# A routed layer's results stored in slot order, gathered again by the attention behind it, and a bias moved from TensorE to VectorE

## Time and profile before

| | us |
|---|---|
| median of 3 runs | 1647.91 (1646.39 to 1648.25) |
| the profiled execution | 1648.63 |
| its span, first to last instruction | 1646.8 |

### The profile page before, as it was taken

The page is one execution under the profiler, slowest core; times in us unless marked ns, Lnnn a source line. Parts: engine busy times, 40 slices in busy tenths (PEclk is TensorE's granted clock), DMA queues, the critical chain, the costliest instruction groups (busy, mean ns, idle before and its releaser), DMA issues. The chain is left out here.

```text
span 1646.8 us, 34410 instructions
## 1 busy us (share of the span) xinstructions
PE 1358.9 (83%) x10706; PEld 1040.7 (63%) x10706; DVE 1048.7 (64%) x3598; ACT 745.1 (45%) x1519; POOL 691.5 (42%) x865
## 2 busy tenths in 40 slices
PE   3899999999849999999999556643888888299997
PEld 1566666666627888888888445532665556188886
DVE  3678777787547888888888636662788877201100
ACT  2445545455327676766767233331333333044332
POOL 2344444443300435353535438882334343234443
PEclk9999999999759999999999779986999999599999
DMA  2222122220030000000000066531400000375550
GB/s 77 34 31 39 21 37 29 28 38 16 12 103 1 17 24 19 19 23 16 26 13 26 17 214 186 174 106 51 129 27 36 29 35 31 136 253 196 182 177 11
DMA packets 65752, 108.62 MB, mean 66 GB/s; under 512 B 9767, under 2 KB 34395, under 8 KB 65296
## 3 DMA queue, kind: packets, MB, share of 16 engines
q1 hardware_dynamic: 54416, 82.27, 19.0%
q0 software_dynamic: 11264, 25.46, 4.3%
HBM read 65.34 MB, written 36.04 MB: 62 GB/s over the span
## 5 line engine op out<-in xcount | busy, mean ns | idle before, releaser
L1124 DVE TENSOR_TENSOR m_Sl<-m_S,m_Sh 128x512 fp32r<-128x512 f32 x256 | 174.3, 690 | 32.4 <-ACT m_S L1034 27.6
L1034 ACT ACTIVATE m_S<-PS,W 128x512 f32<-128x512 f32 x256 | 175.7, 686 | 25.5 <-PE PS L942 22.5
L1570 PE MATMUL PS<-f_xT,f_wt 128*128 128x256 f32 x480 | 123.3, 394 | 42.8 <-ACT f_xT L1606 42.8
L1378 POOL DMA_INDIRECT rows<-r_row,r_posi x128 | 130.5, 1019 | 35.7 <-issue 35.7
L1365 POOL TENSOR_TENSOR r_soft<-r_euler,r_soft 128x32 f32<-128x32 f32 x16 | 86.8, 5428 | 133.2 <-DVE r_soft L1270 133.2
L1029 ACT ACTIVATE m_Sh<-PS,W 128x512 fp32r<-128x512 f32 x128 | 88.2, 689 | 106.2 <-PE PS L942 105.9
L735 DVE TENSOR_TENSOR am<-PS,C 128x512 f32<-128x512 f32 x192 | 119.4, 676 | 20.9 <-PE PS L427 20.9
L1581 PE MATMUL PS<-f_wt,f_hid 128*128 128x128 f32 x960 | 130.9, 279 | 1.8 <-ACT f_hid L1619 1.8
L1655 DVE TENSOR_TENSOR f_res<-PS,f_row 128x256 f32<-128x256 f32 x40 | 17.0, 424 | 181.1 <-PE PS L1585 181.1
L1581 PEld LDWEIGHTS PS<-f_wt,f_hid 128*128 128x128 f32 x960 | 122.7, 191 | 11.1 <-ACT f_hid L1619 2.0
L1570 PEld LDWEIGHTS PS<-f_xT,f_wt 128*128 128x128 f32 x480 | 87.2, 195 | 58.5 <-ACT f_xT L1606 35.6
(11 more groups left out here) (233 smaller groups left out, 3280.9 us busy)
## 6 DMA issues: line engine op xcount, KB each, us to landing
f_row<-rows SPq DMA_DIRECT2D x80, 260.0 KB, 2.7
f_wt<-wr SPq DMA_DIRECT2D x40, 514.0 KB
f_wt<-wr SPq DMA_DIRECT2D x40, 256.0 KB, 3.1
rows<-r_padding SPq DMA_DIRECT2D x32, 260.0 KB, 3.2
X<-x SPq DMA_DIRECT2D x16, 256.0 KB, 5.6
qr<-qphi SPq DMA_DIRECT2D x64, 64.0 KB
kr<-kphi SPq DMA_DIRECT2D x64, 64.0 KB
X<-mid SPq DMA_DIRECT2D x16, 256.0 KB, 2.9
```

The costliest lines, as they stand in the source:

```text
L1034: nc.scalar.activation(S[:, n % 3, :], PS[:, n % 3, :], ACT.Silu, bias=w("b1")[:, n:n + 1]).then_inc(s_ready, 1)
L1124: nc.vector.tensor_tensor(Sl[:, n % 4, :], S[:, n % 3, :], Sh[:, n % 4, :].bitcast(F32), ALU.subtract).then_inc(sl_ready, 1)
L1378: nc.gpsimd.indirect_dma_start(out=self.rows, out_offset=bass.IndirectOffsetOnAxis(ap=self.posi[:, u, t:t + 1], axis=0), in_=self.row[:, u ...
L1570: mm = nc.tensor.matmul(PS[:, 2 + 2 * (u % 2) + bank, half * SLOT:(half + 1) * SLOT], wt[:, u, f * P:(f + 1) * P], xT[:, u % 2, :], start= ...
```

## The change

Five parts go together.

1. Layer 0's rows are 132 floats instead of 260: normalised X and the gate factor. X and the token number aren't sent; ACT's copy and DVE's copy of the number stay in layer 1 only.
2. Layer 0's results are stored in slot order by SP: in the step of slot s, SP first waits for the result of slot s-8 and stores it to rows (s-8)*256 and on of `mid`, then it issues the loads of slot s. The last 8 stores follow the loop. POOL stores nothing in this layer; DVE casts no tokens and adds beta in the closing step, without X.
3. DVE keeps each token's place (`where.row`) in `dve_place`, and at the start of the first routed layer turns it into its position in slot order (`find_tokens`, five operations).
4. The softmax attention's X stays in SBUF. POOL fetches the results of a batch by four indirect DMAs (gathers) into `G`, two batches ahead, between its two variance steps and its scatters; DVE adds G to X ahead of the statistics. SP's loads of X are gone.
5. Layer 1: b2 is part of the weights, repeated for all 128 partitions (514 KB become 578 KB a slot). The bias row's DMA, the row of ones and the two bias products a slot are gone; DVE adds row and bias into `xb` before it waits for PE, then PE's output to xb.

```diff
-ROW = 260
+ROW = (132, 260)
@@ mixture, ACT
-                    if n == 15:
-                        route(routing.act_copy_x, act, p)
@@ Routing.dve_place
+        if not self.layer:
+            nc.vector.tensor_copy(self.where.row[:, bass.ds(b * CT, CT)], self.pos[:, :])
@@ Routing.pool_scatter
-        pool.wait_ge(self.x_copied, b + 1)
+        if self.layer:
+            pool.wait_ge(self.x_copied, b + 1)
@@ routed, SP
+            def store(s, u):
+                sp.wait_ge(res_ready, s + 1)
+                sp.dma_start(dest[bass.ds(s * SLOT, SLOT), :].rearrange("(p a) d -> p a d", a=2), res[:, u, :, :]).then_inc(stored[u], 16)
+
             def step(s, u, turn):
+                if not layer and since(s, DEPTH):
+                    store(s - DEPTH if isinstance(s, int) else s + (-DEPTH), u)
                 r = sp.value_load(slot_row[0:1, bass.ds(s, 1)], min_val=0, max_val=ROWS - SLOT)
                 e = sp.value_load(slot_expert[0:1, bass.ds(s, 1)], min_val=0, max_val=EXPERTS - 1)
-                if since(s, DEPTH):
+                if layer and since(s, DEPTH):
                     sp.wait_ge(res_ready, s - (DEPTH - 1))
                 sp.dma_start(row[:, u, :, :], rows[bass.ds(r, SLOT), :].rearrange("(p a) r -> p a r", a=2)).then_inc(rows_in[u], 16)
                 sp.dma_start(wt[:, u, :], weights[bass.ds(e, 1), :, :].rearrange("o p n -> (o p) n")).then_inc(weights_in[u], 16)
-                if layer:
-                    sp.dma_start(b2r[0:1, u, :], b2[bass.ds(e, 1), :]).then_inc(weights_in[u], 16)
             over_slots(sp, step)
+            if not layer:
+                for u in range(DEPTH):
+                    store(NSLOT - DEPTH + u, u)
+                for u in range(DEPTH):
+                    sp.wait_ge(stored[u], 16 * NSLOT // DEPTH)
@@ routed, POOL
                 inverse_deviation(s, u % 2)
-                if since(s, 1):
-                    store(s - 1 if isinstance(s, int) else s + (-1), (u - 1) % DEPTH)
             over_slots(pool, step)
-            if not layer:
-                store(NSLOT - 1, DEPTH - 1)
@@ routed, PE
-                    if layer:
-                        mm = nc.tensor.matmul(PS[:, 6 + v, a * P:(a + 1) * P], one_row[:, :], b2r[0:1, u, :],
-                                              start=False, stop=True)
@@ routed, DVE
-            def add_x(s, u):
+            def add_x(s, u, turn):
+                v = u % 2
+                dve.wait_ge(weights_in[u], 16 * (turn + 1))
+                if since(s, 2):
+                    dve.wait_ge(res_ready, s - 1)
+                nc.vector.tensor_tensor(xb[:, v, :, :], row[:, u, :, COL_X:COL_X + P],
+                                        wt[:, u, B2:B2 + P].unsqueeze(1).to_broadcast([P, 2, P]), ALU.add).then_inc(xb_ready, 1)
+                dve.wait_ge(xb_ready, s + 1)
                 dve.wait_ge(out_psum, s + 1)
-                nc.vector.tensor_tensor(res[:, u, :, :], PS[:, 6 + u % 2, 0:SLOT].rearrange("p (a d) -> p a d", a=2),
-                                        row[:, u, :, COL_X:COL_X + P], ALU.add).then_inc(res_ready, 1)
+                nc.vector.tensor_tensor(res[:, u, :, :], PS[:, 6 + v, 0:SLOT].rearrange("p (a d) -> p a d", a=2),
+                                        xb[:, v, :, :], ALU.add).then_inc(res_ready, 1)
+
+            def find_tokens(dve):
+                by_tile = [P, TILES, EXPERTS]
+                nc.vector.tensor_scalar(where.limit[:, :], c("region"), float(REGION), None, ALU.add).then_inc(found, 1)
+                dve.wait_ge(found, 1)
+                nc.vector.tensor_tensor(where.passed[:, :, :], where.row[:, :].unsqueeze(2).to_broadcast(by_tile),
+                                        where.limit[:, :].unsqueeze(1).to_broadcast(by_tile), ALU.is_ge).then_inc(found, 1)
+                dve.wait_ge(found, 2)
+                nc.vector.tensor_tensor(where.passed[:, :, :], where.passed[:, :, :],
+                                        where.jump[:, :].unsqueeze(1).to_broadcast(by_tile), ALU.mult).then_inc(found, 1)
+                dve.wait_ge(found, 3)
+                nc.vector.tensor_reduce(where.back[:, :], where.passed[:, :, :], AX.X, ALU.add).then_inc(found, 1)
+                dve.wait_ge(found, 4)
+                nc.vector.tensor_tensor(where.index[:, 0:TILES], where.row[:, :], where.back[:, :], ALU.subtract).then_inc(found, 1)
@@ routed, DVE, statistics(s, u) and close(s, u, turn)
-                nc.vector.tensor_tensor(xb[:, v, :, :], row[:, u, :, COL_X:COL_X + P],
-                                        w("beta").unsqueeze(1).to_broadcast([P, 2, P]), ALU.add).then_inc(xb_ready, 1)
+                if since(s, DEPTH):
+                    dve.wait_ge(stored[u], 16 * turn)
...
-                                                         xb[:, v, a, :], ALU.mult, ALU.add)
+                                                         w("beta"), ALU.mult, ALU.add)
@@ softmax_attention, SP
-            for b in range(BATCHES):
-                if b:
-                    sp.wait_ge(x_in, 16 * b)
-                sp.dma_start(X[:, b * CT:(b + 1) * CT, :],
-                             mid[b * SEQ:(b + 1) * SEQ, :].rearrange("(c p) d -> p c d", p=P)).then_inc(x_in, 16)
-            sp.wait_ge(x_in, 16 * BATCHES)
@@ softmax_attention, POOL
+            def fetch(b, u):
+                if not isinstance(b, int) or b >= 2:
+                    pool.wait_ge(added, b + (-1))
+                nc.gpsimd.tensor_copy(where_now[:, u, :], where.index[:, bass.ds(b * CT, CT)]).then_inc(located, 1)
+                pool.wait_ge(located, b + 1)
+                nc.gpsimd.tensor_tensor(told[:, :], minus_half[:, :], minus_half[:, :], ALU.mult).then_inc(told_done, 1)
+                for t in range(CT):
+                    nc.gpsimd.indirect_dma_start(
+                        out=G[:, u, t, :], out_offset=None, in_=mid,
+                        in_offset=bass.IndirectOffsetOnAxis(ap=where_now[:, u, t:t + 1], axis=0)).then_inc(fetched[u], 16)
+
             def a(b, u, nxt, sent):
-                for step in sent[:1] + nxt + sent[1:]:
+                for step in sent[:1] + nxt:
                     step()
+                if not isinstance(b, int) or b < BATCHES - 1:
+                    fetch(b + 2, u)
+                for step in sent[1:]:
+                    step()
+            fetch(0, 0)
+            fetch(1, 1)
             routing.pool_begin(pool)
@@ softmax_attention, DVE
                 def stats():
-                    dve.wait_ge(x_in, 16 * b + 16)
+                    dve.wait_ge(fetched[u], 8 * CT * b + 8 * CT * (2 - u))
+                    xb = X[:, bass.ds(b * CT, CT), :]
+                    nc.vector.tensor_tensor(xb, xb, G[:, u, :, :], ALU.add).then_inc(added, 1)
+                    wait_apart(dve, nc, added, b + 1, scratch)
```

More of the change, by code:

```diff
@@ L39 @@
 NO_TOKEN = 9000.0
+@dataclass
+class SimpleWhere:
+    index: object
+    row: object
+    jump: object
+    passed: object
+    limit: object
+    back: object
 WCOLS = {}
@@ L91, in program @@
         slot_expert = sb("slot_expert", [P, NSLOT], I32)
+        where = SimpleWhere(index=sb("where_index", [P, TILES + CT], I32), row=sb("where_row", [P, TILES]),
+                            jump=sb("where_jump", [P, EXPERTS]), passed=sb("where_passed", [P, TILES, EXPERTS]),
+                            limit=sb("where_limit", [P, EXPERTS]), back=sb("where_back", [P, TILES]))
         PS = ctx.enter_context(nc.psum_tensor("PS", [P, 8, 512], F32))
@@ L808, in _, with mixture @@
             stages(dve, steps)
-def mixture(nc, sems, X, w, c, PS, before, ones, minus_half, eps, scratch, H, LG, w1t, w2t, rows, slot_row, slot_expert, scattered):
+def mixture(nc, sems, X, w, c, PS, before, ones, minus_half, eps, scratch, H, LG, w1t, w2t, rows, slot_row, slot_expert, where, scattered):
     with ExitStack() as ctx:
@@ L853, in mixture @@
         N = MOE * MOE_CHUNKS
-        routing = Routing(0, ctx, nc, sems, X, w, c, PS, before, ones, minus_half, eps, scratch, rows, slot_row, slot_expert,
+        routing = Routing(0, ctx, nc, sems, X, w, c, PS, before, ones, minus_half, eps, scratch, rows, slot_row, slot_expert, where,
                           bank=5, scattered=scattered, x_ready=x_ready)
@@ L1136, with __init__ @@
 class Routing:
-    def __init__(self, layer, ctx, nc, sems, X, w, c, PS, before, ones, minus_half, eps, scratch, rows, slot_row, slot_expert,
+    def __init__(self, layer, ctx, nc, sems, X, w, c, PS, before, ones, minus_half, eps, scratch, rows, slot_row, slot_expert, where,
                  bank, scattered, x_ready):
@@ L1162, in __init__ @@
         self.rstd = sb("rstd", [P, CT])
[L1163 removed]
+        self.row = sb("row", [P, buffers, CT, width])
         self.xT = sb("xT", [P, SEQ])
@@ L1221, in dve_begin @@
         nc.vector.tensor_copy(self.base[:, :], self.c("region")).then_inc(self.place_step, 1)
-        nc.vector.memset(self.row[:, :, :, COL_TV:ROW], 0.0).then_inc(self.place_step, 1)
+        if not self.layer:
```

(15 more changed lines are left out.)

68 lines of the change are left out of this document (40 added, 28 removed).

## The result

The changed kernel takes 1569.38 us (median of 4 runs, 1567.54 to 1570.3) against 1647.61 us (1646.39 to 1648.25) for the kernel before on the same chip: ratio 0.9525, 95% interval 0.9508 to 0.9541. The forecast was 1586.0 with a range of 1572 to 1608: faster, as said, and 16.6 us more so, outside the range.

A forecast was written before the change was run, and what follows sets the result against it. Limits: POOL in the first routed layer, no full engine in softmax attention, PE in the second layer. -35 + 7.2 + 1.4 - 35.5 = -61.9; 1648.63 - 61.9 - 0.7 = 1586.0 us, range 1572 to 1608.

The forecast's parts named there:

- I take 0.90 a slot: Second layer: PE's gain without its two bias products, period 4.90 to 4.0 us, -35.5 us for the stage.
- all of the rest: Second layer: upper bound of the gain, 0.93 us a slot, given as -38 us for the stage.
- Rival 1: Second layer: a bias product is worth only a full one, 0.27 us, 21.6 in place of 35.5: 1600 us; 8%.
- a change of accumulation group: Second layer: 0.15 us of each bias product's 0.42 might belong to this, stay and reappear.
- SP's step: First layer: SP's three-DMA step sets the pace, 3.25 us for 24 loop steps, 2.95 for the last 8.
- the landing: First layer: time from the issue of the last row's load until it has landed, 2.7 us.
- the exit: First layer's end: from SP's last store to the next stage's first POOL instruction, 4.7 us with 0.4 for the issue.
- POOL's ring: First layer before the change: POOL's variance step, barrier multiply and two indirect stores limit the slot to 3.69 us.
- Softmax, start: Softmax attention: two sets of four gathers put POOL's first variance step at 11.8 us against 4.6, +7.2; bounds +5 and +11.
- Softmax, steady: Softmax attention: gathers hidden, DVE's 0.72 us add covered by its wait for POOL except in the first two batches, +1.4.
- Rival 4: Softmax attention: gathers dearer than scatters make POOL the limit, slower than before, 1665 us at 3.3 us a gather; 4%.
- Rival 6: First layer: SP's loop step near its lower bound, 2.85 us, 12.4 us less, 1574; 5%.

The follow-up runs named there:

- a2: The kernel before with each second-layer bias product made over all 128 rows (ones in row 0, zeros below) instead of one: 1621.70 us, ratio 0.9839.
- a1: The kernel before with the second layer's bias products left out, the bias not added, its DMA kept: 1600.87 us, ratio 0.9712.
- d1: The kernel before with the two bias products of a slot put one behind the other, nothing left out: 1634.55 us, ratio 0.9923.
- b3: The changed kernel with G loaded by plain SP DMAs in slot order instead of gathers, so the tokens aren't their own: 1560.58 us, ratio 0.9467.
- b1: The changed kernel with the first layer's 40 stores issued by ACT, four slots late, instead of by SP: 1551.51 us, ratio 0.9412.
- b4: The changed kernel with POOL's second set of gathers moved behind its first variance step: 1566.94 us, ratio 0.9508.
- b2: The changed kernel with a second DVE add of the same size (zeros to X) behind the add of G: 1573.28 us, ratio 0.9544.

## Why the prediction was right in mechanism and wrong in size

- **Second layer, the failed step: "I take 0.90 a slot".** It measured 1.17, and 39 x 0.27 = 10.5 us are the whole difference of this stage. The step priced a bias product by the distance from its own start to the next (0.42) and took 0.1 more as possibly its own, with 0.93, "all of the rest", as the upper bound. The bound was false: it took the four products behind a bias product (1.09) as the undisturbed pace, and they were slowed too. Undisturbed they take 0.89 (a2). The earlier trace rows held the sign of it: the four products ahead took 0.98, but the 1.09 of those behind was taken as it stood. (By the section's own sum 0.93 gives -36.7, not -38.) Rival 1 took the product for a full one, 0.27, and erred the other way: a1 and a2 give 0.585 for one row against 0.223 for 128. The Trainium skill has the rule beside it ("TensorE: Matmul & The Clock Gate", section "Why this matters for your kernels": a single product over 32 rows takes as long as one over 128). d1 doesn't contradict it for the product by itself, since only some 0.03 us stayed with the products once two changes were gone; what it leaves out is the change, and between full products the rule is of no use. The prediction's other thought, that a change of accumulation group might be what costs, falls with a2, which has the same groups and not the price. PE has no gap and the other engines follow at 3.73, as forecast.
- **First layer, -41.4 for -35; the failed steps are SP's step, the landing and the exit.** SP's steps replaced POOL's ring, PE waits for rows at nearly each slot and POOL is 31% busy, as said. The steps: loop 3.12 for 3.25 (24 x 0.13 = 3.0), last eight 2.88 for 2.95 (0.6), landing 2.1 for 2.7 (0.6), last result 10.2 us behind it for 10. The exit took 2.2 for 4.7, 2.5 us. What SP waited for at the two ends says where it went, in the kernel before at the row that the 4.7 was taken from the earlier trace rows and then in the changed kernel behind its last store (us in all, times, longest; PEq is PE's instruction list):

```profile
SPq L1705 <- DMA rows<-r_padding: 2.1, 1, 2.1
SPq L1705 <- PEq L1705: 2.0, 1, 2.0
```

```profile
SPq L1553 <- DMA mid<-f_res: 1.1, 1, 1.1
SPq L1481 <- PEq L1481: 0.2, 1, 0.2
```

About 1.0 us is the landing, of one small store in place of paddings; the larger part, 1.8, is that PE's instruction list came to the block's end 2.0 us behind the landing before, and 0.2 now. At the end of the softmax stage this wait for PE is 2.0 to 2.8 us in every kernel without gathers (the kernel before, its five variants and b3) and 0.2 in every kernel with them, the same paddings before both. Why stays open. b1 confirms the limit.
- **Softmax, start: +7.6 for +7.2.** A gather of 128 rows takes POOL 0.95 us, as the scatter that stood in for it. b3 and b4 confirm that the start is the gathers' queue on POOL.
- **Softmax, steady.** The forecast had 0 but for the first two batches, +1.4; up to the first scatter it was +0.8. The add was covered, as b2 shows; but 13 of the 15 steps between scatters grew by 0.26, of which 0.20 is DVE slowed beside the gathers (b3), a term that the forecast put at nothing: +3.4. The stage's end is 1.8 us shorter, since SP waits 0.2 for PE's list and not 2.0 (L1752, the same eight paddings ahead of it); no step of the forecast had that. Together with the start it is +10.0 for +8.6, nearer than the steps deserve. Rival 4 (gathers that make POOL the limit) was far off: POOL keeps 3.42 us.
- **Mixture, -1.3 for 0**, inside its bounds of -2 and +1; not tested, and no more than the scatter of that part between profiled runs.

The errors add up to 10.5 + 6.4 + 1.3 - 1.4 = 16.8, and three of the four lie on one side. The lower end, 1572, is 14 below the forecast: it held each of them, but not the two largest together. Rival 6, the shorter SP step, came true at a third of its size at the same time.

## What to carry to other kernels

Price an operation that is taken out not by its own row but by the pace of its neighbours where it is absent: find the same neighbours undisturbed (here four products in 0.89 us) before you call a bound one. Where a short product has to stand among full ones, filling its contraction up to 128 rows with zeros gave 27 us here, and putting the short ones side by side 14. Where a single engine issues all DMAs of a stage, count its DMAs a step before its bytes, and give one of them to an engine with time to spare. Work moved to a less busy engine can still sit at the stage's start, where nothing covers it: issue there only what the first step needs.

## What the runs showed of the hardware

- Between fp32 products over 128 rows and one over 1 or 64 rows, each change costs PE 0.17 to 0.18 us (d1: two changes fewer, 0.33 less; a2: four fewer, 0.72 less), and at a change the weight load doesn't start ahead of its product as it does elsewhere (by 0.11 us). A product over one row between full ones cost 0.585 us in all where a full one takes 0.223.
- An indirect gather of 128 rows of 512 bytes occupies POOL for 0.95 us and 0.30 between two, as an indirect scatter does.
- A step of SP that reads its two addresses from a table takes 2.2 to 2.5 us with two DMAs (the kernel before's first layer, b1) and 2.9 to 3.3 with three (its second layer, the changed kernel's first).
- DVE's 128x128 normalise `s_xn` takes 387 ns in place of 340 while POOL runs copies and gathers (b3).
- From SP's last padding to the next stage's first instruction it was 4.3 us in the kernel before and 2.6 in the changed one, with the same eight paddings: at such an end it pays to read what the last engine waits for.
